# Scores of tiles 2 to 7 built on the bank's last tile from differences of key blocks, in a two-layer attention kernel on one core

## The chip, the cores and the metric

One core of a Trainium2 chip runs the whole program. The metric is the device time of one execution in microseconds; the median of the runs is given. The engines named here are TensorE (PE, with its weight loads as PEld), VectorE (DVE), ScalarE (ACT), GpSimd (POOL) and SyncE (SP), which issues most transfers. Each engine works through its own list of instructions in order; semaphores tie the lists together.

## The reference

Four images of 64 channels and 32 x 32 positions go through two layers. Each layer is a group norm, a single-head self-attention over the 1024 positions, and a residual:

```python
h = group_norm(x, norm_w, norm_b)             # 32 groups
q, k, v = h @ Wq + bq, h @ Wk + bk, h @ Wv + bv
scores = einsum('bnc,bmc->bnm', q, k) * C ** (-0.5)   # C = 64
attn = softmax(scores, axis=-1)
x = x + (einsum('bnm,bmc->bnc', attn, v) @ Wo + bo)
```

## The kernel before

A unit is one image in one layer: UNITS = 8, and LAST = 7. The 1024 positions are held as two halves of 512 (HALF), one half in partitions 0 to 63 and the other in 64 to 127, with the channels along the partitions. The scores of a unit are made transposed, 128 keys by 1024 queries at a time: TILES = 8 tiles, each filling two PSUM banks (left: queries of one half, right: of the other). JS = 4 blocks of 128 positions make a half.

The projection (`project`, L741) puts queries and keys of one half into each of two buffers: `front` holds queries of the first half in its upper 64 partitions and keys of it in its lower, `back` keys of the second half above and queries below. So that queries and keys stand in the same partitions, SP copies halves of them into `cross` (`swap_hi`, `swap_lo`). Products are made in a reduced float format; to keep the precision, each operand is split in a high part (written by ScalarE, L389 to L398) and a low part, the rest (VectorE, L557 and L564; for units 0 and 1 GpSimd, L307). A tile of scores (`scores_main`, L791) is three pairs of matmuls, high by high, high by low and low by high; a pair works on the upper and the lower 64 rows of the array, for the left and the right bank.

To each tile a fourth pair (`scores_row`, L821) adds the row of negated maxima, `q_row`, through a matrix of ones, so that the exponential on ScalarE (`exp`, L440) finds scores less the query's maximum. The maxima come one unit ahead: while unit w has its scores made, `next_max(w, m)` (L724) makes one plain high-by-high product for unit w+1, `part` (L571) on VectorE reduces it over keys, `join` (L595) takes the last step, `turn_max` (L783) transposes the result on TensorE, `stage_max` copies it, and SP puts it in `q_row` (`place_rows`, L240).

The order is written out by hand for each engine. One pass w over the steady loop:

- TensorE (L950): `next_max` and `scores` of tiles 0 to 7 in turn, the denominators of unit w-1 (L865), `values` (probabilities by values, L833) of tiles 0 to 4, a wait for `rden_done`, `turn_max(w+1)`, values 5 and 6, `project(w+2)`, `project_v(w+2)`, values 7. Two score buffers alternate, so tile t waits for exponential t-2. The last unit (L986) has three buffers and no maxima to make.
- VectorE (L687): the eight reductions `part`, with `first_add` (sum of probabilities of tiles 0 and 1) among them, `join`, statistics of unit w+2 (`own_stats`, `share_stats`, `join_stats`), the reciprocal of unit w-1's denominators, `affine`, `low_front` and `low_back` of unit w+2.
- ScalarE (L478): eight exponentials, the norm, `stage_max`, `bias_x`, `high_front`, `high_back`, `copy_v`, `copy_attn`.
- GpSimd (L344): the sums of probabilities of tiles 2 to 7 (`add`, L317), with `root` (L301, for the norm of unit w+2) after the third of them, and `finish(w-1)` before the last.
- SP (L274): spread of the reciprocal, `place_rows`, then the four `cross` transfers of unit w+2.

Of the kernel before, what the change touches and what calls it, by code (L numbers as in the profile page):

```python
# [11 lines left out]
P = 128  # L12
# [18 lines left out]
def attention_pair(nc, x, layer_params, consts, out):  # L31
# [14 lines left out]
    JS = HALF // P  # L46
    POOL_ADDS = TILES - 2
# [4 lines left out]
    with ExitStack() as ctx:  # L52
# [13 lines left out]
        back_w = [sb(f"back_w{n}", [P, P]) for n in range(LAYERS)]  # L66
        back_bias = [sb(f"back_bias{n}", [P, 1]) for n in range(LAYERS)]
# [17 lines left out]
        front = [sb(f"front{b}", [P, N], F32R) for b in range(RING)]  # L85
        back = [sb(f"back{b}", [P, N], F32R) for b in range(RING)]
        cross = [sb(f"cross{b}", [P, N], F32R) for b in range(RING)]
        full_front = sb("full_front", [P, HALF])
        full_back = sb("full_back", [P, HALF])
# [33 lines left out]
        back_set = sem("back_set")  # L123
# [10 lines left out]
        front_hi = sem("front_hi")  # L134
        back_hi = sem("back_hi")
        front_full = sem("front_full")
        back_full = sem("back_full")
        front_lo = sem("front_lo")
        back_lo = sem("back_lo")
        first_back_hi = sem("first_back_hi")  # L140
        head_front_lo = sem("head_front_lo")
        head_back_lo = sem("head_back_lo")
# [3 lines left out]
        hi_swapped = [sem(f"hi_swapped{b}") for b in range(RING)]  # L146
        lo_swapped = [sem(f"lo_swapped{b}") for b in range(RING)]
# [40 lines left out]
        def low_count(later, head, unit):  # L188
            return (head, unit + 1) if unit < HEAD else (later, unit + 1 - HEAD)
# [7 lines left out]
        HI, LO = slice(0, HALF), slice(HALF, N)  # L197

        def back_hi_of(unit):
            return (back_hi, unit) if unit else (first_back_hi, 1)  # L200
# [13 lines left out]
        def scores_buffer(unit, t):  # L214
            return ps_scores[t % 2] if unit < LAST else (ps_scores[0], ps_scores[1], ps_max)[t % 3]
# [4 lines left out]
        def _(sp):  # L220
# [4 lines left out]

            def swap_hi(u):
                t = cross[u % RING]
                sp.wait_ge(front_hi, u + 1)
                sp.dma_start(t[0:C, HI].bitcast(F32), front[u % RING][C:P, HI].bitcast(F32)).then_inc(hi_swapped[u % RING], 16)
                sp.wait_ge(*back_hi_of(u))  # L230
                sp.dma_start(t[C:P, HI].bitcast(F32), back[u % RING][0:C, HI].bitcast(F32)).then_inc(hi_swapped[u % RING], 16)

            def swap_lo(u):
                t = cross[u % RING]
                sp.wait_ge(*low_count(front_lo, head_front_lo, u))
                sp.dma_start(t[0:C, LO].bitcast(F32), front[u % RING][C:P, LO].bitcast(F32)).then_inc(lo_swapped[u % RING], 16)
                sp.wait_ge(*low_count(back_lo, head_back_lo, u))
                sp.dma_start(t[C:P, LO].bitcast(F32), back[u % RING][0:C, LO].bitcast(F32)).then_inc(lo_swapped[u % RING], 16)
# [32 lines left out]
            for u in range(2):  # L271
                swap_hi(u)
                swap_lo(u)
            for w in range(UNITS):  # L274
                if 0 < w < LAST:
                    spread_rden(w - 1)
                if w + 1 < UNITS:
                    place_rows(w + 1)
                if w == LAST:
                    spread_rden(w - 1)  # L280
                if w + 2 < UNITS:
                    swap_hi(w + 2)
                    swap_lo(w + 2)
                if w > B:
                    store(w - 1 - B)
# [4 lines left out]
        def _(pool):  # L290
# [16 lines left out]
            def low_parts(u):  # L307
                pool.wait_ge(front_hi, u + 1)
                pool.wait_ge(front_full, u + 1)
                pool.tensor_tensor(front[u][:, LO], full_front[:, :], front[u][:, HI].bitcast(F32),  # L310
                                   ALU.subtract).then_inc(head_front_lo, 1)
                pool.wait_ge(*back_hi_of(u))
                pool.wait_ge(back_full, u + 1)
                pool.tensor_tensor(back[u][:, LO], full_back[:, :], back[u][:, HI].bitcast(F32),
                                   ALU.subtract).then_inc(head_back_lo, 1)
# [26 lines left out]
            low_parts(0)  # L342
            low_parts(1)
# [9 lines left out]
        def _(act):  # L353
# [6 lines left out]
            def set_back(n):  # L360
                act.wait_ge(params_in[n], 16)
                low = slice(C, P)
                act.activation(back_w[n][low, 0:C], layer[n][low, WK:WK + C], ACT.Copy)
                act.activation(back_w[n][low, C:P], layer[n][low, WQ:WQ + C], ACT.Copy)
                act.activation(back_bias[n][0:C, :], layer[n][low, BIAS_QK:BIAS_QK + 1], ACT.Copy)
                act.activation(back_bias[n][low, :], layer[n][0:C, BIAS_QK:BIAS_QK + 1], ACT.Copy).then_inc(back_set, 1)
# [22 lines left out]
            def high_front(u):  # L389
                act.wait_ge(params_in[u // B], 16)  # L390
                act.wait_ge(proj_mm, u + 1)
                act.activation(front[u % RING][:, HI], projected(u)[:, HI], ACT.Identity,  # L392
                               bias=layer[u // B][:, BIAS_QK:BIAS_QK + 1]).then_inc(front_hi, 1)

            def high_back(u):
                act.wait_ge(back_set, u // B + 1)
                act.activation(back[u % RING][:, HI], projected(u)[:, LO], ACT.Identity,
                               bias=back_bias[u // B][:, :]).then_inc(back_hi, 1)  # L398

            def whole_front(u):  # L400
                if u:
                    act.wait_ge(head_front_lo, u)
                act.activation(full_front[:, :], ps_scores[0][:, HI], ACT.Identity,
                               bias=layer[u // B][:, BIAS_QK:BIAS_QK + 1]).then_inc(front_full, 1)

            def whole_back(u):
                if u:
                    act.wait_ge(head_back_lo, u)
                else:
                    act.wait_ge(first_back_hi, 1)  # L410
                act.wait_ge(back_set, u // B + 1)
                act.activation(full_back[:, :], ps_scores[0][:, LO], ACT.Identity,
                               bias=back_bias[u // B][:, :]).then_inc(back_full, 1)
# [47 lines left out]
            set_back(0)  # L461
            apply_norm_first()
            high_front(0)
            whole_front(0)
            whole_back(0)
            apply_norm(1)
            copy_v(0)
            set_back(1)
            high_front(1)
            high_back(1)  # L470
            whole_front(1)
            whole_back(1)
# [5 lines left out]
            for w in range(UNITS):  # L478
                prep = w + 2 < UNITS
                for t in range(TILES):  # L480
                    exp(w, t)
                if prep:
                    apply_norm(w + 2)
# [573 lines left out]
```

## Time and profile before

| | |
|---|---|
| median of 3 runs | 180.64 us (180.60 to 180.78) |
| the profiled execution | 180.29 us, of which the span is 178.5 |
| TensorE, VectorE, GpSimd, ScalarE busy | 96%, 78%, 67%, 57% of the span |
| a steady unit | 20.06 us |

The page gives each engine's busy time as a share of the span. A timeline lists instructions by start and duration in us, a run of like ones in one row ("x8" with the time from the first start to the last end); in square brackets stands how long the engine had been idle, and whose work ended that. Matmuls follow each other before the one in front has ended, so the spacing of their starts, not their duration, is what each costs. VectorE and ScalarE instructions overlap by about 0.1 us in the same way.

### The profile page before, as it was taken

To read this page: it belongs to the slowest core of one execution; us is meant where nothing else is said; L and a number is where in the kernel's file an instruction comes from. 1 tells how busy PE (TensorE), PEld (TensorE's weight loads), DVE (VectorE), ACT (ScalarE), POOL (GpSimd) and SP (SyncE) were. 2 spreads that over 40 slices of the span, in tenths; PEclk is the share of its full clock that TensorE was granted. 3 is DMA by queue.
4 is the path that set the end of the run, shared out by engine and by line. 5 is a ranking of instruction groups with operands and counts; after the bars stand their busy time and mean duration, and the time that the engine had idled before them with its cause. 6 is when DMAs were issued, how large, how long until landed. Compare 5 with 4: busy or idle time off the path is not lost.

```text
span 178.5 us, 3311 instructions
## 1 busy us (share of the span) xinstructions
PE 170.8 (96%) x1239; PEld 92.5 (52%) x1239; DVE 139.0 (78%) x201; ACT 102.6 (57%) x137; POOL 119.2 (67%) x78
## 2 busy tenths in 40 slices
PE   7868899999999999999999999999999999999992
PEld 3425575247632665247632665247632665358671
DVE  2799899539993899739992899739992899979943
ACT  3479388257923786167923786167923786039400
POOL 3265029893889879888889879888889879700000
PEclk9999999999999999999999999999999999999999
DMA  5544200004001500034001500034001510113011
GB/s 147 207 88 92 59 0 0 2 19 105 0 4 46 130 3 4 0 74 103 4 0 48 128 5 0 0 76 107 0 0 49 131 62 0 32 33 102 16 62 59
DMA packets 6656, 8.90 MB, mean 50 GB/s; under 512 B 1208, under 2 KB 3696, under 8 KB 6640
## 3 DMA queue, kind: packets, MB, share of 16 engines
q1 hardware_dynamic: 6208, 8.23, 18.7%
q10 hardware_dynamic: 432, 0.46, 0.8%
q8 instruction: 10, 0.16, 0.4%
q14 instruction: 6, 0.05, 0.1%
HBM read 1.58 MB, written 1.05 MB: 15 GB/s over the span
## 4 chain that ended last, share of the span: by engine, by line
PE 88%; DVE 7%; DMA 1%; issue 1%; POOL 0%; ACT 0%; DVEq 0%; POOLq 0%
PE ps_both L846 28%; PE ps_scores L814 9%; PE ps_scores L830 8%; PE ps_scores L816 8%; PE ps_scores L818 8%; PE ps_max L771 5%; DVE part_max L576 4%; PE ps_both L853 4%; PE ps_scores L750 4%; PE ps_both L758 3%; PE ps_both L771 3%; PE ps_both L871 2%; PE ps_scores L771 2%; DMA xs<-x_dram 1%; PE ps_both L785 1%
## 5 line engine op out<-in xcount | busy, mean ns | idle before, releaser
L324 POOL TENSOR_TENSOR prob_sum<-prob_sum,probs 128x1024 f32<-128x1024 f32 x40 | 95.1, 2378 | 20.8 <-DVE prob_sum L606 17.6
L450 ACT ACTIVATE probs<-ps_scores 128x1024 f32<-128x1024 f32 x62 | 63.3, 1027 | 12.9 <-PE ps_scores L831 6.5
L846 PE MATMUL ps_both<-probs,vals 128*64 128x512 f32 x224 | 52.2, 598 | 0.0
L576 DVE TENSOR_REDUCE part_max<-ps_max 128x2 f32<-128x1024 f32 x32 | 39.1, 1223 | 1.1 <-PE ps_max L772 0.4
L846 PEld LDWEIGHTS ps_both<-probs,vals 128*64 128x64 f32 x224 | 14.6, 136 | 24.1 <-issue 23.0
L576 DVE TENSOR_REDUCE part_max<-ps_both 128x2 f32<-128x1024 f32 x21 | 25.7, 1224 | 0.8 <-PE ps_both L772 0.7
L830 PE MATMUL ps_scores<-q_row,ones_r 64*128 64x512 f32 x62 | 24.4, 393 | 0.5 <-ACT q_row L432 0.5
L831 PE MATMUL ps_scores<-q_row,ones_r 64*128 64x512 f32 x62 | 24.4, 394 | 0.0
L559 DVE SCALAR_TENSOR_TENSOR front<-ps_scores,layer,front 128x512 fp32r<-128x512 f32 x6 | 4.5, 750 | 23.5 <-ACT front L392 23.5
L381 ACT ACTIVATE h<-xs,shift,gain 128x512 f32<-128x512 f32 x7 | 5.7, 811 | 26.8 <-DVE shift L543 26.8
L576 DVE TENSOR_REDUCE part_max<-ps_scores 128x2 f32<-128x1024 f32 x11 | 13.4, 1223 | 1.1 <-PE ps_scores L772 1.1
L830 PEld LDWEIGHTS ps_scores<-q_row,ones_r 64*128 64x128 f32 x62 | 11.4, 184 | 3.2 <-issue 0.7
L614 DVE RECIPROCAL quarter_rden<-ps_both 128x256 f32<-128x256 f32 x7 | 12.2, 1750 | 1.0 <-PE ps_both L871 1.0
L814 PE MATMUL ps_scores<-front,back 64*128 64x512 f32 x31 | 12.9, 415 | 0.0
L815 PE MATMUL ps_scores<-back,cross 64*128 64x512 f32 x31 | 12.8, 414 | 0.0
L815 PE MATMUL ps_scores<-back,front 64*128 64x512 f32 x31 | 12.3, 398 | 0.0
L814 PE MATMUL ps_scores<-front,cross 64*128 64x512 f32 x31 | 12.3, 398 | 0.0
L818 PE MATMUL ps_scores<-front,back 64*128 64x512 f32 x31 | 12.1, 391 | 0.0
L819 PE MATMUL ps_scores<-back,front 64*128 64x512 f32 x31 | 12.1, 391 | 0.0
L819 PE MATMUL ps_scores<-back,cross 64*128 64x512 f32 x31 | 12.1, 391 | 0.0
L818 PE MATMUL ps_scores<-front,cross 64*128 64x512 f32 x31 | 12.1, 391 | 0.0
L817 PE MATMUL ps_scores<-back,front 64*128 64x512 f32 x31 | 12.1, 390 | 0.0
(161 smaller groups left out, 393.8 us busy)
## 6 DMA issues: line engine op xcount, KB each, us to landing
cross<-front SPq DMA_DIRECT2D x16, 128.0 KB, 2.3
cross<-back SPq DMA_DIRECT2D x16, 128.0 KB, 2.3
rden<-quarter_rden SPq DMA_DIRECT2D x28, 64.0 KB, 2.1
xs<-x_dram SPq DMA_DIRECT2D x4, 256.0 KB, 4.7
out_dram<-xs SPq DMA_DIRECT2D x3, 256.0 KB, 3.2
q_row<-max_rows SPq DMA_DIRECT2D x14, 2.0 KB
layer<-layers_dram SPq DMA_DIRECT2D x1, 194.5 KB, 2.7
layer<-layers_dram ACTq DMA_DIRECT2D x1, 194.5 KB, 4.7
```

The costliest lines, as they stand in the source:

```text
L324: pool.tensor_tensor(total[:, :], total[:, :], probs[t][:, :], ALU.add).then_inc(added, 1)
L450: act.activation(probs[t][:, :], scores_buffer(u, t)[:, :], ACT.Exp, scale=SCALE).then_inc(exp_done, 1)
L576: dve.tensor_reduce(part_max[u % 2][:, at:at + 2 * JS + 1:2 * JS], ps[:, :].rearrange("p (g n) -> p g n", g=2), AX.X, ALU.max, negate=True ...
L771: pe.matmul(ps[:, HI], f[top, tile], (x if crossed else g)[top, HI], start=True, stop=True)
L814: pe.matmul(left, key_top[top, hi], front_u[top, HI], start=True, stop=False)
L815: pe.matmul(right, key_low[low, hi], back_u[low, HI], start=True, stop=False)
L816: pe.matmul(left, key_top[top, hi], front_u[top, LO], start=False, stop=False)
L818: pe.matmul(left, key_top[top, lo], front_u[top, HI], start=False, stop=False)
L819: pe.matmul(right, key_low[low, lo], back_u[low, HI], start=False, stop=False)
L830: pe.matmul(left, ones_r[top, :], row[top, :], start=False, stop=True)
L831: pe.matmul(right, ones_r[low, :], row[low, :], start=False, stop=True).then_inc(scores_mm, 1)
L846: mm = pe.matmul(ps_attn[half * C:(half + 1) * C, :], v, probs[t][:, cols], start=(t == 0), stop=(t == TILES - 1))
```

## The change

Softmax of a query does not change when a tile's scores are taken as the last tile's scores plus a product with the difference of two key blocks. From unit 1 on, tiles 0 and 1 are made as before (anew, with the row of maxima). Tiles 2 to 7 start from what the bank still holds, the tile two back, and add the product of the queries with the difference between their key block and that one: three pairs of matmuls with no start flag, and no fourth pair. Tiles now alternate between the two halves of the keys, from the last block down (`key_block`).

For this, keys and queries get buffers of their own: `q_hi`, `q_lo`, `k_hi` and `k_lo` hold both halves, queries or keys of the first half in one set of 64 partitions and of the second in the other; `x_hi` and `x_lo` hold the keys exchanged. `k_hi` and `x_hi` have 384 columns more (DIFF = HALF - P) for the differences. `project` makes four products of 64 rows by 64 columns in place of two of 64 by 128. ScalarE makes one more copy per unit, `whole_keys` (keys in full precision), and `high_differences` after the exponentials. VectorE makes `key_differences` (384 columns) in place of `low_back`, and, one pass later and just ahead of the reciprocal, `low_keys`. SP moves the exchange of the low parts to the next pass, ahead of the reciprocal's spread, and adds the exchange of the differences. The last unit has two score buffers in place of three, and its values are set between its scores. Unit 0 keeps its row of maxima in all tiles.

```diff
@@ SP
-            for u in range(2):
-                swap_hi(u)
-                swap_lo(u)
+            def swap_hi(u):
+                sp.wait_ge(*k_hi_of(u))
+                exchange(x_hi[u % RING], k_hi[u % RING], HI, hi_swapped[u % RING])
+            def swap_differences(u):
+                sp.wait_ge(d_hi_set, u)
+                exchange(x_hi[u % RING], k_hi[u % RING], DIFFS, d_swapped[u % RING])
+            def swap_lo(u):
+                sp.wait_ge(*k_lo_of(u))
+                exchange(x_lo[u % RING], k_lo[u % RING], HI, lo_swapped[u % RING])
...
+            swap_hi(0)
+            swap_lo(0)
+            swap_hi(1)
             for w in range(UNITS):
+                if w + 1 < UNITS:
+                    swap_differences(w + 1)
+                    swap_lo(w + 1)
                 if 0 < w < LAST:
                     spread_rden(w - 1)
...
                 if w + 2 < UNITS:
                     swap_hi(w + 2)
-                    swap_lo(w + 2)
@@ ACT
+            def whole_keys(u):
...
+                act.activation(k_full[u % 2][:, HI], projected(u)[:, LO], ACT.Identity,
+                               bias=bias_k[u // B][:, :]).then_inc(k_full_set, 1)
+            def high_differences(u):
+                act.wait_ge(*diff_of(u))
+                act.activation(k_hi[u % RING][:, DIFFS], k_full[u % 2][:, DIFFS], ACT.Copy).then_inc(d_hi_set, 1)
...
                 for t in range(TILES):
                     exp(w, t)
+                if w < LAST:
+                    high_differences(w + 1)
                 if prep:
                     apply_norm(w + 2)
...
-                    high_front(w + 2)
-                    high_back(w + 2)
+                    high_queries(w + 2)
+                    high_keys(w + 2)
+                    whole_keys(w + 2)
                     copy_v(w + 2)
@@ DVE
+            def key_differences(u):
+                full = k_full[u % 2]
+                dve.wait_ge(k_full_set, u + 1)
+                dve.scalar_tensor_tensor(out=full[:, DIFFS], in0=projected(u)[:, HALF:HALF + DIFF],
+                                         scalar=bias_k[u // B][:, :], in1=full[:, P:HALF],
+                                         op0=ALU.add, op1=ALU.subtract).then_inc(diff_set, 1)
+            def low_keys(u):
+                dve.wait_ge(k_hi_set, u)
+                dve.wait_ge(d_hi_set, u)
+                dve.tensor_tensor(k_lo[u % RING][:, :], k_full[u % 2][:, CHAIN], k_hi[u % RING][:, CHAIN].bitcast(F32),
+                                  ALU.subtract).then_inc(k_lo_set, 1)
...
                     join_stats(w + 2)
+                low_keys(w + 1)
                 if w:
                     reciprocal(w - 1)
                 if prep:
                     affine(w + 2)
-                    low_front(w + 2)
-                    low_back(w + 2)
+                    low_queries(w + 2)
+                    key_differences(w + 2)
@@ PE
-                pe.matmul(projected(u)[:, HI], p[first, 0:P], h[first, :], start=True, stop=True)
-                pe.wait_ge(back_set, u // B + 1)
-                pe.matmul(projected(u)[:, LO], back_w[u // B][second, :], h[second, :], start=True, stop=True).then_inc(proj_mm, 1)
+                pe.matmul(ps[TOP, HI], p[TOP, wq], h[TOP, :], start=True, stop=True)
+                pe.matmul(ps[LOW, HI], p[LOW, wq], h[LOW, :], start=True, stop=True)
+                pe.matmul(ps[LOW, LO], p[TOP, wk], h[TOP, :], start=True, stop=True)
+                pe.matmul(ps[TOP, LO], p[LOW, wk], h[LOW, :], start=True, stop=True).then_inc(proj_mm, 1)
...
             def scores(u, t):
                 scores_main(u, t)
-                scores_row(u, t)
+                if u == 0 or t < 2:
+                    scores_row(u, t)
...
+                product(left, top_hi[TOP, hi], q_hi[b][TOP, :], anew, False)
+                product(right, low_hi[LOW, hi], q_hi[b][LOW, :], anew, False)
+                product(left, top_hi[TOP, hi], q_lo[b][TOP, :], False, False)
+                product(right, low_hi[LOW, hi], q_lo[b][LOW, :], False, False)
+                product(left, top_lo[TOP, lo], q_hi[b][TOP, :], False, not anew)
+                mm = product(right, low_lo[LOW, lo], q_hi[b][LOW, :], False, not anew)
+                if not anew:
+                    mm.then_inc(scores_mm, 1)
...
-            for t in range(TILES):
+            for t in range(4):
                 scores(LAST, t)
             pe.wait_ge(rden_done, LAST)
             values(LAST, 0)
             values(LAST, 1)
+            scores(LAST, 4)
+            scores(LAST, 5)
             values(LAST, 2)
             values(LAST, 3)
-            denominators_last()
+            scores(LAST, 6)
+            scores(LAST, 7)
             values(LAST, 4)
             values(LAST, 5)
+            denominators_last()
             spread_last()
             values_last(0)
             values_last(1)
```

## Rows read from the trace of the kernel before

**Rows 1.** The page: busy time, share of the span, instructions of each engine.

```profile
PE 170.8 (96%) x1239; PEld 92.5 (52%) x1239; DVE 139.0 (78%) x201; ACT 102.6 (57%) x137; POOL 119.2 (67%) x78
```

**Rows 2.** Timeline, VectorE, one steady unit: start, duration, instruction, idle time before.

```profile
60.30 1.23 DVE L576 TENSOR_REDUCE part_max<-ps_max 128x2 f32<-128x1024 f32 x1
...
63.76 1.22 DVE L606 TENSOR_TENSOR prob_sum<-probs 128x1024 f32<-128x1024 f32 x1
64.89 1.22 DVE L576 TENSOR_REDUCE part_max<-ps_both 128x2 f32<-128x1024 f32 x1
...
69.80 1.23 DVE L576 TENSOR_REDUCE part_max<-ps_scores 128x2 f32<-128x1024 f32 x1 [0.16 <-PE ps_scores L772]
71.06 0.17 DVE L599 TENSOR_REDUCE neg_max<-part_max 128x8 f32<-128x16 f32 x1
...
73.00 1.75 DVE L614 RECIPROCAL quarter_rden<-ps_both 128x256 f32<-128x256 f32 x1
...
78.83 0.75 DVE L559 SCALAR_TENSOR_TENSOR front<-ps_scores,layer,front 128x512 fp32r<-128x512 f32 x1 [3.87 <-ACT front L392]
79.50 0.74 DVE L566 SCALAR_TENSOR_TENSOR back<-ps_scores,back_bias,back 128x512 fp32r<-128x512 f32 x1
80.36 1.23 DVE L576 TENSOR_REDUCE part_max<-ps_max 128x2 f32<-128x1024 f32 x1
```

**Rows 3.** Timeline, TensorE, the same unit.

```profile
60.80 0.39 PE L830 MATMUL ps_scores<-q_row,ones_r 64*128 64x512 f32 x1
...
61.03 0.39 PE L771 MATMUL ps_both<-back,front 64*128 64x512 f32 x1
...
70.26 4.51 PE L846 MATMUL ps_both<-probs,vals 128*64 128x512 f32 x20
74.80 0.27 PE L785 MATMUL ps_both<-const_sb,neg_max 128*8 128x128 f32 x1
...
76.87 0.69 PE L750 MATMUL ps_scores<-h,layer 64*128 64x512 f32 x1
...
77.93 1.09 PE L758 MATMUL ps_both<-wvo,h 128*64 128x128 f32 x16
```

**Rows 4.** Timeline, ScalarE, the same unit.

```profile
61.24 9.15 ACT L450 ACTIVATE probs<-ps_scores 128x1024 f32<-128x1024 f32 x8 [0.77 <-PE ps_scores L831]
...
78.11 0.69 ACT L392 ACTIVATE front<-ps_scores,layer 128x512 fp32r<-128x512 f32 x1 [1.49 <-PE ps_scores L752]
78.69 0.68 ACT L397 ACTIVATE back<-ps_scores,back_bias 128x512 fp32r<-128x512 f32 x1
```

**Rows 5.** Timeline, GpSimd and VectorE, unit 6.

```profile
145.40 9.92 POOL L324 TENSOR_TENSOR prob_sum<-prob_sum,probs 128x1024 f32<-128x1024 f32 x4 [1.28 <-DVE prob_sum L606]
...
153.11 3.29 DVE L630 TENSOR_TENSOR late_sum<-probs 128x1024 f32<-128x1024 f32 x1
```

**Rows 6.** Timeline, GpSimd, the steady unit.

```profile
65.11 7.44 POOL L324 TENSOR_TENSOR prob_sum<-prob_sum,probs 128x1024 f32<-128x1024 f32 x3 [1.24 <-DVE prob_sum L606]
73.04 0.55 POOL L305 TENSOR_TENSOR rstd<-var_eps,minus_half 128x1 f32<-128x1 f32 x1 [0.48 <-DVE var_eps L530]
```

**Rows 7.** Timeline, the last unit, all engines.

```profile
158.50 0.50 PE L814 MATMUL ps_scores<-front,cross 64*128 64x512 f32 x1
...
159.74 1.95 ACT L450 ACTIVATE probs<-ps_scores 128x1024 f32<-128x1024 f32 x2 [1.09 <-PE ps_scores L831]
...
166.07 3.67 PE L853 MATMUL ps_both<-probs,vals 128*64 128x256 f32 x32
...
169.51 0.69 DVE L652 TENSOR_TENSOR attn<-attn,rden 128x512 f32<-128x512 f32 x1
...
170.88 0.96 DVE L616 RECIPROCAL block_rden<-ps_max 128x128 f32<-128x128 f32 x1
...
172.53 1.04 PE L895 MATMUL ps_max<-block_rden,const_sb 128*64 128x128 f32 x16
```

## What the change is predicted to do, and why

> **What bounds the kernel now.** I read the page first, then the timelines of one steady unit (from 60 to 80 us), engine by engine, then the last two units. TensorE is 96% busy and VectorE 78% [rows 1], so the page alone says that TensorE matmuls taken away are time won. The unit says otherwise. Follow VectorE from the first reduction of one unit to the first of the next [rows 2, 3, 4]: reductions and the first add 60.30 to 71.06 (10.76 us), join and statistics to 73.00 (1.94), reciprocal until TensorE may turn the maxima at 74.80 (1.80), two value tiles until the projection at 76.87 (2.07), projection until ScalarE's first copy at 78.11 (1.24), copies and low parts until the next first reduction at 80.36 (2.25): 20.06 us, one closed loop. TensorE's own work is as long: its five value tiles end at 70.26 + 4.51 = 74.77, just when the turn (held by rden_done) is released [rows 3]. Whoever shortens one of the two only meets the other.
>
> **What TensorE gains.** A pair of row matmuls takes the slot from 60.80 to 61.03, 0.23 us [rows 3]. Six tiles lose it: 6 x 0.23 = 1.39 us per unit. Tiles 2 to 7 still wait for the exponential two tiles back, and the eight exponentials, 9.15 us now [rows 4], come somewhat faster. So TensorE reaches the turn about 1 us earlier, and is then held there by the reciprocal.
>
> **What VectorE's loop gains and loses, per unit.**
> - Reductions: now and then they wait for TensorE, 0.16 us in front of the last one [rows 2]; that is the least gain. The spacing of operations that wait for nothing is 1.13 us (63.76 to 64.89). Eight at that and 1.26 for the last (69.80 to 71.06) make 10.30: at most 0.46 gained. I take 0.35, since TensorE will be ahead nearly everywhere.
> - low_keys is new, between the statistics and the reciprocal, so in the loop. Two SBUF inputs of 512 columns: half of the 1.13 of the 1024-column add is 0.57, and the spacing of the present low part of 512 columns is 0.67 (78.83 to 79.50) [rows 2]. I take 0.60, with nobody in its way (below).
> - key_differences takes low_back's place, but waits for k_full, a third ScalarE copy. Copies follow at 0.58 (78.11, 78.69) [rows 4]: the third starts at 79.27, and with 0.68 ends at 79.95. A column costs about 1 ns (1.13 us for 1024), so 384 columns cost 0.13 less than 0.67, and reductions can start at 79.97 + 0.54 = 80.51 for 80.36: +0.15 (0 to +0.3).
> - The same copy pushes copy_v and copy_attn back, behind which next_max 1 and the first exponential stand: copy_attn ends at 78.11 + 4 x 0.58 + 0.60 = 81.03, and next_max 1 comes some 1.2 us after the first reduction's matmuls, at about 81.1. Nothing, with little to spare.
> - high_differences runs on ScalarE after the last exponential (61.24 + 9.15 = 70.39), when it idles; d_hi is there before VectorE asks at 73.0. Nothing.
> - SP: the exchanges of differences and low keys now stand ahead of the reciprocal's spread and of the q_row transfers. low_keys ends 1.75 us before the reciprocal does, time for two issues, and some 6 us remain until scores read what they bring. Nothing.
> - Projection: four 64x64 matmuls for two 64x128. The present two, on different rows, run together: 76.87 to 77.93, 1.06 us for both in two passes. Value matmuls, on different columns, run together too: 20 in 4.51, 0.23 each, where one projection pass takes 0.53 [rows 3]. No row shows rows and columns both split. Bounds: 0 (four at once) and +1.06 (two pairs in turn). I take 0, since each of the four has its own quarter of the array.
>
> By the Trainium skill ("TensorEngine Tiling (Array Packing)", Tiling Modes) 64x64 gives four independent tiles, but its Gotcha 1 (PSUM Pressure) says that different row tiles cannot access one PSUM bank at once, and the two query products do write one bank. No row here has that pattern; by that rule the projection would take at least a turn more, as in rival 3.
>
> Sum: -0.35 + 0.60 + 0.15 + 0 = +0.40 us per unit.
>
> **The port between VectorE and GpSimd.** The one present operation of VectorE with two SBUF inputs that meets a GpSimd add in full is the tail's pair sum: 3.29 us from 153.11 to 156.40, while four GpSimd adds run from 145.40 to 155.32 [rows 5]; the same shape takes 1.22 elsewhere [rows 2]. 155.32 + 1.08 = 156.40: it was not slowed down, it waited for the add to end. low_keys is such an operation. In a steady unit GpSimd's third add ends at 72.55 and its root starts at 73.04 [rows 6]; low_keys would start where the reciprocal does now, at 73.00 [rows 2]. With the reductions 0.35 shorter it comes 9.24 - 0.35 = 8.9 us after first_add's start, the third add ends 8.8 us after it, and root, set off by the same statistics, still follows some 0.04 behind low_keys. It slips in and root waits for it, which costs nothing: root has time till the reciprocal is over. So 0.60 stands, but by a hair.
>
> The Trainium skill ("SBUF — State Buffer", SBUF: two separate sides) calls this an exclusive lock, held by whichever of a two-input VectorE operation and a GpSimd operation starts first. The tail row agrees (a wait of 2.2 us); by that rule, too, low_keys is first by 0.04 us.
>
> **The ends.** Head and unit 0: VectorE's reductions follow each other there as before, low_keys runs ahead of a norm that is not last, and only the +0.15 stays. Units 1 to 5: 5 x 0.40 = 2.0. Unit 6 has no statistics, so low_keys falls into the third of its four adds (2.48 each) [rows 5] and waits for its end at 152.84 + 0.15; it then holds the fourth up by 0.6, to 156.1. The pair sum (1.08) and the tail add (1.22) follow, so denominators and scores come about 0.6 late, 0.15 of it counted: +0.45. Last unit [rows 7]: six row pairs gone, -1.39; two buffers for three, so tile 2 waits for exponential 0 (159.74 + 1.03 + 0.07 = 160.84, +0.38) and tile 3 for exponential 1 (161.69, +0.22). Value tiles 4 and 5 now stand ahead of the denominators, and nothing covers the reciprocal. From the first score: tiles 0 to 3 end at 3.95, value tiles 0 and 1 (3.67 for four) at 5.8, scores 4 and 5 at 7.2, value tiles 2 and 3 at 9.0; exponential 6 starts 0.9 later and ends at 10.9. The last late add ends at 12.15, finish_tail takes 1.37 (169.51 to 170.88), the reciprocal 0.96: the spread starts at 14.5, for 172.53 - 158.50 = 14.03 now: +0.5 net.
>
> Total: 0.15 + 2.0 + 0.45 + 0.5 = +3.1 us. The sum is made on the profiled execution, 180.29 us with a span of 178.5; the median of the runs is 180.64, 0.35 more, and a difference carries over: 180.64 + 3.1 = 183.7. With the bounds but port and projection: +0.11 to +0.8 per unit and 0.2 to 1.3 at the ends, so 181.5 to 185.9.
>
> **Rivals.**
> 1. GpSimd first at the port. For it: 0.04 us decides. If root (0.55 [rows 6]) gets in, low_keys waits for it: +0.55 in five units, 2.75, 186.5 us. If the add behind root gets in too, 0.55 + 2.48 per unit: 5 x 3.0 and about 4 in units 0 and 6, some 203 us. Against the second: VectorE is already waiting when the port falls free.
> 2. Faster: the reductions follow TensorE, so their stretch shrinks by the full 1.39. Then -1.39 + 0.60 + 0.15 = -0.64 per unit, -3.2, with +1.1 at the ends 178.5 us. It decides once the stretch loses over 0.75 us, that is when eight spacings fall to 1.09 us. For it: the spacings look like TensorE's tile, five pairs of 0.23. Against it: the add at 63.76 to 64.89 waits for no maxima, and takes 1.13 as well.
> 3. The projection in two turns: +1.06 in six units, 6.4, so 190.1 us. For it: no row shows the pattern. Against it: column and row splits each run side by side.
> 4. That the change does not do what it says can only mean that tiles 2 to 7 get no shorter, because the wait for the exponential holds them. TensorE has slack at the turn, so the time is the forecast's.
>
> **How the numbers follow.** Forecast 50% (183.7, from 181.5 to 185.9); rival 1 short 17%, long 5%; rival 3 14%; rival 2 9%; gains and losses cancel, 5%. A measurement of this kernel tells about 0.2%, 0.36 us, from no change. Faster 9%, same 5%, slower 86%. The forecast, short rival 1 and rival 3 hold 81%: 181.5 to 190.2.
>
> **What the profile will show.** TensorE idle about 1 us ahead of the turn, released by the reciprocal; low_keys at 0.6 us between mean_gain and reciprocal (near 1.2: root was first; over 3: an add was); the projection's slot at 1.06 or at 2.1; a period near 20.5 us; reductions 1.13 apart without waits; TensorE idle ahead of the last spread. A period under 20.06 us, or a turn that the reciprocal doesn't release, would make the prediction wrong.

## The result and the profile after

The changed kernel takes 185.05 us (median of 4 runs, 184.82 to 185.17) where the kernel before, run beside it, takes 180.71 (180.60 to 180.88): a ratio of 1.0242, with a 95% interval of 1.0222 to 1.0263. It is slower by 4.3 us, and the forecast was +3.1 (183.7, range 181.5 to 190.2). The profiled execution took 184.93 us with a span of 183.1, 4.6 more than the span of before.

The page of the changed kernel, busy time by engine and the shares of the chain that ended last. TensorE was 96% busy [rows 1] and is 91%, and VectorE now carries half of the chain, where TensorE carried 88% of it:

```profile
PE 166.4 (91%) x1187; PEld 84.9 (46%) x1187; DVE 141.8 (77%) x208; ACT 106.8 (58%) x150; POOL 121.5 (66%) x78
...
DVE 50%; PE 29%; issue 8%; ACT 6%; DMA 2%; SPq 2%; POOL 0%; DVEq 0%; ACTq 0%; POOLq 0%
```

The chain of the kernel before, for comparison:

```profile
PE 88%; DVE 7%; DMA 1%; issue 1%; POOL 0%; ACT 0%; DVEq 0%; POOLq 0%
```

Timeline, VectorE, the same steady unit as [rows 2]:

```profile
61.04 1.22 DVE L623 TENSOR_REDUCE part_max<-ps_max 128x2 f32<-128x1024 f32 x1
...
71.46 0.17 DVE L646 TENSOR_REDUCE neg_max<-part_max 128x8 f32<-128x16 f32 x1
...
73.40 0.81 DVE L615 TENSOR_TENSOR k_lo<-k_full,k_hi 128x512 fp32r<-128x512 f32 x1
74.13 1.75 DVE L661 RECIPROCAL quarter_rden<-ps_both 128x256 f32<-128x256 f32 x1
...
81.10 0.62 DVE L608 SCALAR_TENSOR_TENSOR k_full<-ps_scores,bias_k,k_full 128x384 f32<-128x384 f32 x1 [0.40 <-ACT k_full L447]
81.63 1.21 DVE L623 TENSOR_REDUCE part_max<-ps_max 128x2 f32<-128x1024 f32 x1
```

Timeline, TensorE, the same unit, to be read against [rows 3]:

```profile
70.35 4.51 PE L910 MATMUL ps_both<-probs,vals 128*64 128x512 f32 x20
75.93 0.27 PE L834 MATMUL ps_both<-const_sb,neg_max 128*8 128x128 f32 x1 [1.07 <-DVE quarter_rden L661]
76.14 1.94 PE L910 MATMUL ps_both<-probs,vals 128*64 128x512 f32 x8
78.00 0.64 PE L798 MATMUL ps_scores<-h,layer 64*64 64x512 f32 x1
78.01 0.64 PE L799 MATMUL ps_scores<-h,layer 64*64 64x512 f32 x1
78.02 0.64 PE L800 MATMUL ps_scores<-h,layer 64*64 64x512 f32 x1
78.03 0.64 PE L801 MATMUL ps_scores<-h,layer 64*64 64x512 f32 x1
...
79.02 1.09 PE L807 MATMUL ps_both<-wvo,h 128*64 128x128 f32 x16
```

The value tiles end at 74.86, and then TensorE stands idle for 1.07 us until the reciprocal lets it turn the maxima: most of the time of the six row pairs lies here (the second run below puts it back). VectorE's loop reads, against before: first reduction to join 10.42 us for 10.76 (-0.34), join to reciprocal 2.67 for 1.94 (+0.73; +0.60 a unit later, where low_keys takes 0.60), reciprocal to projection 3.87 for 3.87, projection to first reduction 3.63 for 3.49 (+0.14). In the unit shown low_keys takes 0.81 because GpSimd's third add still runs until 73.65. Over the four steady units from 61.04 to the first reduction of unit 6 at 143.01 the period is 20.49, for 20.07 before.

The port between VectorE and GpSimd, one unit later: low_keys and the root of the next norm (for [rows 6]). low_keys starts 0.04 us ahead; the root, 0.55 before, takes 1.05:

```profile
93.97 0.68 DVE L615 TENSOR_TENSOR k_lo<-k_full,k_hi 128x512 fp32r<-128x512 f32 x1
94.57 1.75 DVE L661 RECIPROCAL quarter_rden<-ps_both 128x256 f32<-128x256 f32 x1
```

```profile
94.01 1.05 POOL L335 TENSOR_TENSOR rstd<-var_eps,minus_half 128x1 f32<-128x1 f32 x1
```

In unit 0 the root is first, by 0.15 us, and neither of the two takes longer (GpSimd, then VectorE):

```profile
33.91 0.55 POOL L335 TENSOR_TENSOR rstd<-var_eps,minus_half 128x1 f32<-128x1 f32 x1 [0.53 <-DVE var_eps L572]
```

```profile
34.06 0.68 DVE L615 TENSOR_TENSOR k_lo<-k_full,k_hi 128x512 fp32r<-128x512 f32 x1
```

GpSimd's last add of a unit and VectorE's first_add of the next: the add ends at 85.06, and first_add starts at 85.13.

```profile
82.66 2.40 POOL L360 TENSOR_TENSOR prob_sum<-prob_sum,probs 128x1024 f32<-128x1024 f32 x1
```

```profile
85.13 1.22 DVE L653 TENSOR_TENSOR prob_sum<-probs 128x1024 f32<-128x1024 f32 x1
```

The ends (for [rows 5] and [rows 7]). VectorE in unit 6, where low_keys and the pair sum wait for adds of a run of four on GpSimd (148.07 to 158.25):

```profile
153.71 2.34 DVE L615 TENSOR_TENSOR k_lo<-k_full,k_hi 128x512 fp32r<-128x512 f32 x1
155.97 1.75 DVE L661 RECIPROCAL quarter_rden<-ps_both 128x256 f32<-128x256 f32 x1
157.63 1.70 DVE L677 TENSOR_TENSOR late_sum<-probs 128x1024 f32<-128x1024 f32 x1
```

SP issues the last unit's row of maxima behind the four spreads:

```profile
160.30 1.31 SPq L274 DMA_DIRECT2D q_row<-max_rows  x2
```

TensorE in the last unit: first score, first row of maxima, tile 2, the first value run, the first scores behind it, the spread:

```profile
161.27 0.49 PE L875 MATMUL ps_scores<-q_hi,x_hi 64*128 64x512 f32 x1
...
162.69 0.49 PE L893 MATMUL ps_scores<-q_row,ones_r 64*128 64x512 f32 x1 [0.46 <-DMA q_row<-max_rows]
...
164.40 0.47 PE L875 MATMUL ps_scores<-q_hi,x_hi 64*128 64x512 f32 x1 [0.28 <-ACT probs L489]
...
166.13 1.95 PE L917 MATMUL ps_both<-probs,vals 128*64 128x256 f32 x16
168.01 0.50 PE L875 MATMUL ps_scores<-q_hi,x_hi 64*128 64x512 f32 x1
...
177.10 1.09 PE L959 MATMUL ps_max<-block_rden,const_sb 128*64 128x128 f32 x16 [1.08 <-DVE block_rden L663]
```

So the 4.6 us of span lie at four landmarks: the first reduction of unit 1 comes 0.48 later (40.70 for 40.22), units 1 to 5 add 1.95 (the first reduction of unit 6 is at 143.01 for 140.58, +2.43 in all), unit 6 adds 0.34 (first score of the last unit 161.27 for 158.50, +2.77 in all), and the last unit takes 15.83 us from first score to spread where it took 14.03: +1.80.

### The profile page after: what moved, and what is told of

The parts are those of the page before. It is cut to its first block, busy times and chain, and to the rows that moved or that the text cites. A ratio compares the mean times of both kernels' runs of the same rounds, so it can differ in the third digit from the quotient of the medians.

```text
span 183.1 us, 3264 instructions
## 1 busy us (share of the span) xinstructions
PE 166.4 (91%) x1187; PEld 84.9 (46%) x1187; DVE 141.8 (77%) x208; ACT 106.8 (58%) x150; POOL 121.5 (66%) x78
## 3 DMA queue, kind: packets, MB, share of 16 engines
HBM read 1.58 MB, written 1.05 MB: 14 GB/s over the span
## 4 chain that ended last, share of the span: by engine, by line
DVE 50%; PE 29%; issue 8%; ACT 6%; DMA 2%; SPq 2%; POOL 0%; DVEq 0%; ACTq 0%; POOLq 0%
DVE part_max L623 28%; PE ps_both L910 9%; PE ps_scores L875 6%; DVE quarter_rden L661 6%; DVE prob_sum L653 4%; PE ps_scores L798 4%; PE ps_both L917 4%; DVE stats L551 2%; ACT q_hi L429 2%; ACT k_full L447 2%; DVE k_full L608 2%; DVE k_lo L615 2%; DMA xs<-x_dram 2%; SPq L284 1%; PE ps_max L820 1%
## 5 line engine op out<-in xcount | busy, mean ns | idle before, releaser
L875 PE MATMUL ps_scores<-q_hi,k_hi 64*128 64x512 f32 x64 | 27.6, 431 | 1.1 <-ACT probs L489 1.1
L875 PE MATMUL ps_scores<-q_hi,x_hi 64*128 64x512 f32 x64 | 27.5, 430 | 0.3 <-ACT probs L489 0.3
L875 PE MATMUL ps_scores<-q_hi,x_lo 64*128 64x512 f32 x64 | 25.0, 391 | 0.0
L875 PE MATMUL ps_scores<-q_hi,k_lo 64*128 64x512 f32 x64 | 25.0, 391 | 0.0
L875 PE MATMUL ps_scores<-q_lo,k_hi 64*128 64x512 f32 x64 | 25.0, 390 | 0.0
L875 PE MATMUL ps_scores<-q_lo,x_hi 64*128 64x512 f32 x64 | 24.9, 390 | 0.0
L875 PEld LDWEIGHTS ps_scores<-q_hi,k_hi 64*128 64x128 f32 x64 | 11.7, 183 | 8.1 <-ACT probs L489 7.4
L875 PEld LDWEIGHTS ps_scores<-q_hi,x_lo 64*128 64x128 f32 x64 | 11.8, 184 | 1.2
L875 PEld LDWEIGHTS ps_scores<-q_hi,k_lo 64*128 64x128 f32 x64 | 11.8, 184 | 1.1
L875 PEld LDWEIGHTS ps_scores<-q_lo,x_hi 64*128 64x128 f32 x64 | 11.9, 185 | 0.4
```

Source lines behind the costliest of these rows:

```text
L875: return pe.matmul(out, keys, queries, start=start, stop=stop, skip_group_check=True)
```

## The experiments

In each run the kernel before ran beside it, at 180.5 to 180.9 us in the median. A period below is the mean of the four units between the first reductions of units 2 and 6. The edits are shown in part, with the lines that matter.

### 1 and 2: lengthen VectorE's loop, give TensorE its work back

```diff
@@ low_keys(u), first run: one reduction of 512 columns ahead of it
+                dve.tensor_reduce(spare[:, :], k_full[u % 2][:, HI], AX.X, ALU.max)
```

> The changed kernel with one more VectorE operation ahead of low_keys: a maximum over 512 columns of k_full (one SBUF input, result unused), some 0.6 us. Theory: the VectorE loop (reductions, statistics, low_keys, reciprocal, turn, projection, copies, back to the reductions) sets the period, so units 1 to 5 get 0.6 us longer each and unit 6 up to 0.6: 185.05 + 3.0 to 3.6 = 188.1 to 188.7 us, period 21.05. Rival, that TensorE or ScalarE sets the period and low_keys lies in a gap: 185.0 to 185.5.

Measured: 189.41 us (1.0487, 1.0456 to 1.0518). The period is 21.05, +0.56 for an operation of 0.60, as expected. The rest, some 1.5 us, came in unit 0: there low_keys, 0.6 later than in the changed kernel, found GpSimd's next add running and waited for it.

The first run, VectorE, then GpSimd, unit 0:

```profile
34.73 2.68 DVE L618 TENSOR_TENSOR k_lo<-k_full,k_hi 128x512 fp32r<-128x512 f32 x1
```

```profile
34.50 7.63 POOL L361 TENSOR_TENSOR prob_sum<-prob_sum,probs 128x1024 f32<-128x1024 f32 x3
```

What is put into VectorE's loop is paid nearly in full (0.56 of 0.60), and rival 1's long price (0.60 becomes 2.68) is real once low_keys comes 0.2 us after the start of an add.

```diff
@@ scores(u, t), second run: the fourth pair is back, with zeros for ones in tiles 2 to 7
-                if u == 0 or t < 2:
-                    scores_row(u, t)
+                scores_row(u, t, ones_r if u == 0 or t < 2 else zero_r)
```

> The changed kernel with the fourth pair of matmuls put back in tiles 2 to 7 of units 1 to 7, with zeros in place of the ones, so that it adds nothing: TensorE's saving is undone, all else stays. Theory: TensorE idles 1.1 us ahead of each turn, so 1.39 us more fill that gap; 0.3 us of it shows, and the reductions get back up to 0.35 us of waiting: +0.3 to +0.65 in units 1 to 6 and +1.39 in the last, 188.2 to 190.4 us. Rival, that TensorE's time counts in full: +1.39 in seven units, 194.8 us.

Measured: 188.59 us (1.0446, 1.0409 to 1.0484); period 20.87, +0.38 for 1.39 us of TensorE work a unit. So of the time that the change takes from TensorE, 1.0 us a unit is worth nothing where it lies; the reductions (10.82 us in place of 10.42) take all that does count.

### 3 and 8: the reciprocal ahead of the statistics

```diff
@@ DVE, both runs (SP: the spread ahead of the low keys' exchange)
                 join(w + 1, neg_max[:, :])
+                if w:
+                    reciprocal(w - 1)
                 if prep:
                     own_stats(w + 2)
...
                 low_keys(w + 1)
-                if w:
-                    reciprocal(w - 1)
@@ POOL, run 8 alone: the last add ahead of finishing unit w-1
-                    if t == 6 and 0 < w < LAST - 1:
+                    if t == 7 and 0 < w < LAST - 1:
                         finish(w - 1)
```

> The changed kernel with VectorE's reciprocal straight after the join, ahead of the statistics and low_keys, and SP's spread of it ahead of the exchange of the low keys. Theory: the turn is then free when TensorE comes, some 1.1 us sooner; the norm, which now waits for the reciprocal's 1.75 and for low_keys, becomes what the projection waits for, some 0.45 us sooner than now: -2.2 in five units, and the last unit's row of maxima comes in time (-0.6): 182.2 to 182.9 us. If the projection followed the turn alone: 185.05 - 5 x 1.0 = 180 us. Rival, that the turn's wait hides behind something else: 185 us.

Measured: 188.48 us (1.0434, 1.0398 to 1.0471), slower by 3.4 than the changed kernel: the gain that was expected did not come. The turn was free when TensorE came, but the statistics, and behind them the root and GpSimd's adds, came later by the reciprocal's length, and first_add met GpSimd's last add. VectorE, two units of the third run, then GpSimd:

```profile
64.41 2.41 DVE L653 TENSOR_TENSOR prob_sum<-probs 128x1024 f32<-128x1024 f32 x1
...
85.63 2.44 DVE L653 TENSOR_TENSOR prob_sum<-probs 128x1024 f32<-128x1024 f32 x1
```

```profile
76.12 1.05 POOL L335 TENSOR_TENSOR rstd<-var_eps,minus_half 128x1 f32<-128x1 f32 x1 [1.42 <-DVE var_eps L572]
...
84.60 2.40 POOL L360 TENSOR_TENSOR prob_sum<-prob_sum,probs 128x1024 f32<-128x1024 f32 x1
```

first_add takes 2.44 in place of 1.22: it starts at 85.63, waits until the add of 84.60 is over at 87.00, and ends 1.07 later. The eighth run keeps the order and moves that add.

> Reciprocal ahead of the statistics as in the third run (188.48 us), and GpSimd's last add of a unit ahead of the two operations that finish the unit before. New theory of that run's loss: later statistics made the root and GpSimd's chain late, so that first_add stood 1.2 us before the port until the last add ended. With the add ahead of the wait for the spread reciprocal, the add ends about 3 us sooner, and first_add meets at most one of the short ones: first_add at 1.2 to 1.5 instead of 2.44 us, period 20.2 to 20.4, 183.3 to 184.6. Rival (the order on VectorE itself costs it, the port nothing): period 21.2, 188.5.

Measured: 182.74 us (1.0118, 1.0087 to 1.0149), 5.7 below the third run with one line of GpSimd's list moved; first_add is back at 1.21 to 1.27, the period 20.06, a little better than expected. That period is the one of the kernel before, and what holds it is the norm: VectorE waits 0.44 us for the root in each unit, since low_keys got in ahead of it (GpSimd, then VectorE):

```profile
74.57 1.05 POOL L335 TENSOR_TENSOR rstd<-var_eps,minus_half 128x1 f32<-128x1 f32 x1 [0.45 <-DVE var_eps L572]
```

```profile
75.65 0.21 DVE L583 TENSOR_SCALAR gain<-rstd,layer 128x1 f32<-128x1 f32 x1 [0.44 <-POOL rstd L335]
```

### 5: low_keys taken away

```diff
@@ low_keys(u)
-                dve.tensor_tensor(k_lo[u % RING][:, :], k_full[u % 2][:, CHAIN], k_hi[u % RING][:, CHAIN].bitcast(F32),
-                                  ALU.subtract).then_inc(k_lo_set, 1)
+                dve.memset(k_lo[u % RING][:, 0:1].bitcast(F32), 0.0).then_inc(k_lo_set, 1)
```

> The changed kernel with low_keys taken away: the low parts of keys and differences are zero in units 1 to 7 (cleared once at the start), and VectorE only sets one column to zero in its place, so nothing of it needs the port. Theory (low_keys' 0.60 us stands in VectorE's loop, and in unit 6 it waits at the port and makes the row of maxima late): period 20.45 - 0.6 = 19.85 us, the same 0.6 in unit 0, the root back at 0.55; unit 6's reciprocal of unit 5 starts about 2.3 us sooner after join, the row is there when the last unit's first tile wants it, -0.6. Together about -4.5: 180.2 to 181.2. Rival (GpSimd's chain of adds or TensorE is the real bound, and low_keys stands in a gap that something else keeps open): period above 20.2 us and 183 us or more.

Measured: 181.27 us (1.0042, 1.0018 to 1.0067). The period is 19.93, so low_keys costs 0.56 a unit; the last unit takes 15.10, with the row there in time. Without low_keys the steady unit is a little shorter than before's 20.07. In unit 0, where 0.6 was expected, low_keys costs nothing: from the join of the maxima to the first reduction of unit 1 it takes 8.77 us with it and without it. That reduction came at 41.00 for 40.70 because the join itself came 0.30 later (32.23 for 31.93); whether the added clearing at the start did that is not shown.

### 6: the third copy

```diff
@@ ACT
-                    high_keys(w + 2)
                     whole_keys(w + 2)
+                    high_of_whole(w + 2)     # rounds k_full in SBUF
```

> The changed kernel with ScalarE's second and third copies exchanged: the keys in full precision come first, the high part is rounded from them in SBUF. Theory (key_differences waits 0.40 us for the third copy, and that is the +0.15 of each unit): it starts right behind the low queries, some 0.5 us sooner, and the first reduction is then held only by TensorE's first maxima product; -0.15 to -0.2 us per unit, period 20.25 to 20.30, six units: 184.0 to 184.3. Rival (the first reduction follows TensorE anyway): 185.05, period 20.45.

Measured: 186.61 us (1.0329, 1.0297 to 1.0361); period 20.74, worse by 0.25. key_differences did start behind the low queries, but the first maxima product needs the high part of the keys, which now comes last:

```profile
81.44 0.61 DVE L612 SCALAR_TENSOR_TENSOR k_full<-ps_scores,bias_k,k_full 128x384 f32<-128x384 f32 x1
82.66 1.23 DVE L627 TENSOR_REDUCE part_max<-ps_max 128x2 f32<-128x1024 f32 x1 [0.61 <-PE ps_max L825]
```

Both readings of the +0.14 were too simple: two chains meet at the first reduction, and the order of the copies only chooses which is late.

### 4 and 7: the last unit

```diff
@@ run 4: all tiles of the last unit anew, with the row and three buffers, values behind all scores
-                anew = u == 0 or t < 2
+                anew = u in (0, LAST) or t < 2
@@ run 7: SP, unit 6
-                if 0 < w < LAST:
+                if 0 < w < LAST - 1:
                     spread_rden(w - 1)
                 if w + 1 < UNITS:
                     place_rows(w + 1)
+                if w == LAST - 1:
+                    spread_rden(w - 1)
```

> The changed kernel with the last unit undone: all its tiles made anew with the row of maxima, three score buffers and the old order of scores, values and denominators. Theory: the last unit took 15.83 us from first score to spread in place of 14.03, 0.6 of it by the late row of maxima, which stays: 15.83 becomes 14.65, -1.2, 183.9 us. Rival, that the lost time there comes from late transfers alone: 185.0 us.

Measured: 184.50 us (1.0217, 1.0174 to 1.0260), and the last unit takes 14.75 (162.02 to 176.77), 1.08 less: as expected in the unit. The total shows half of it: in the profiled execution the first reduction of unit 1 came at 41.47 (40.70 in the changed kernel), though the run changes nothing in the head.

> The changed kernel with one exchange in SP's list, in unit 6 alone: the row of maxima of the last unit goes out ahead of the spread of unit 5's reciprocal. Theory (the row, behind four spreads, holds the last unit's first tile by 0.6 us): TensorE's idle time ahead of the first row product goes to 0, last unit from first score to spread 15.83 - 0.6 = 15.2 us, 184.4 to 184.6. Unit 5's output and the reciprocal of unit 6 come about 1.9 us later, with room. Rival (two buffers and the exponentials hold the last unit, and the late row only fills a wait that is there anyway): 185.0, last unit 15.8.

Measured: 185.12 us (1.0266, 1.0208 to 1.0323): no gain. The row came in time and tile 2 started at 163.69 for 164.40, but the spread of unit 5's reciprocal, now last, held the reciprocal of unit 6 until 164.00 (161.88 before the move), and VectorE's late adds became the bound:

```profile
164.00 1.76 DVE L663 RECIPROCAL quarter_rden<-ps_both 128x256 f32<-128x256 f32 x1 [3.40 <-DMA rden<-quarter_rden]
...
168.27 6.54 DVE L695 TENSOR_TENSOR prob_sum<-prob_sum,probs 128x1024 f32<-128x1024 f32 x5
```

The expectation had said "with room". In the fifth and the eighth run, where row and reciprocal both come early, the last unit takes 15.10 and 15.13: the late row is worth 0.7 of its 1.80, and the fourth run puts the other 1.1 on two buffers, the interleaved order and anew against chained tiles together, without telling them apart.

### 9 to 12: use TensorE's idle time

```diff
@@ PE, runs 9 to 12 (run 12: in the kernel before); the POOL line of run 8 in 9, 11 and 12
+                values(w, 5)
+                values(w, 6)
                 if w:
                     pe.wait_ge(rden_done, w)
                 turn_max(w + 1)
-                values(w, 5)
-                values(w, 6)
@@ run 11 alone: the fourth run's last unit, and in unit 6 the reciprocal and its spread
@@ ahead of low_keys and their exchange
```

> The changed kernel with two moves in hand-written order: TensorE does value tiles 5 and 6 ahead of the turn of the maxima (they fill the 1.07 us in which it waited for the reciprocal), and GpSimd adds its last tile ahead of finishing the unit before. Theory (TensorE's gain lies idle ahead of the turn, and the reciprocal holds the projection only through the order turn, value tiles, projection): turn at about 76.7 on the scale of the unit at 61.04, projection right behind, 1.0 us sooner; period 19.4 to 19.8 us, 5 units, 181.0 to 182.0. Rival (GpSimd's chain of six adds, root and two finishing operations takes the bound over, its loop is 19.8 to 20.4): 182.5 to 184.5.

Measured: 181.24 us (1.0020, 1.0002 to 1.0037), 3.8 below the changed kernel; period 19.83, just above what was expected. TensorE, the ninth run: no wait at the turn, and the projection now waits for the norm, 0.28 us here and about 0.15 in the units behind.

```profile
69.32 6.23 PE L910 MATMUL ps_both<-probs,vals 128*64 128x512 f32 x28
75.48 0.27 PE L834 MATMUL ps_both<-const_sb,neg_max 128*8 128x128 f32 x1
76.03 0.64 PE L798 MATMUL ps_scores<-h,layer 64*64 64x512 f32 x1 [0.28 <-ACT h L418]
```

From join to projection it takes 5.53 us in place of 6.54; 0.36 of that goes back at the port, where first_add takes 1.58 behind GpSimd's finishing operation, which runs from 62.43 to 63.72:

```profile
63.22 1.58 DVE L653 TENSOR_TENSOR prob_sum<-probs 128x1024 f32<-128x1024 f32 x1
```

GpSimd's move alone was not run; first_add waits for nothing in the steady units of the changed kernel (1.21), so these rows show nothing there for it to win.

> The same with TensorE's move alone, GpSimd's order left as in the changed kernel. Theory (first_add then comes 1 us sooner, while the last add, held behind the wait for the spread reciprocal, still runs): first_add waits at the port for 0.9 to 1.2 us in each unit, as in the third run, period 20.2 to 20.5, 184.0 to 185.2: the gain of the move is given back. Rival (first_add gets the port at no cost): as in the run before, 181 to 182.

Measured: 184.37 us (1.0196, 1.0158 to 1.0234), period 20.29. Without GpSimd's move most of the gain is given back at the port, as expected: first_add takes 2.04. VectorE, then GpSimd:

```profile
63.93 2.04 DVE L653 TENSOR_TENSOR prob_sum<-probs 128x1024 f32<-128x1024 f32 x1
```

```profile
62.49 2.39 POOL L360 TENSOR_TENSOR prob_sum<-prob_sum,probs 128x1024 f32<-128x1024 f32 x1
...
66.11 4.92 POOL L360 TENSOR_TENSOR prob_sum<-prob_sum,probs 128x1024 f32<-128x1024 f32 x2 [1.23 <-DVE prob_sum L653]
```

> Both moves, the last unit made anew with its row of maxima and three buffers as in the fourth run, and in unit 6 the reciprocal of unit 5 ahead of low_keys. Theory: the gains add, since each was measured at another place: units as in the ninth run, last unit 15.83 - 1.08 - 0.70 = 14.05 us, so 1.8 below the ninth run: 179.0 to 180.3, a little under the kernel before (180.6). Rival (unit 6 is held by GpSimd's adds and the tail, and takes up what the last unit gains): 180.5 to 181.5.

Measured: 179.69 us (0.9942, 0.9919 to 0.9964), 0.6% below the kernel before. The period is 19.83 again, and the last unit 14.06 from first score to spread:

```profile
157.84 0.50 PE L886 MATMUL ps_scores<-q_hi,x_hi 64*128 64x512 f32 x1
...
171.90 1.04 PE L970 MATMUL ps_max<-block_rden,const_sb 128*64 128x128 f32 x16
```

> The kernel before with the same two moves as the ninth run (value tiles 5 and 6 ahead of the turn, last add ahead of the finish). Theory (there TensorE has no idle time ahead of the turn, its own work is as long as the loop): no gain, period 20.0 to 20.1, 180.4 to 181.0; the move only pays with the TensorE time that the change sets free. Rival (the move pays by itself): 178 or less.

Measured: 180.25 us (0.9964, 0.9938 to 0.9990): a small gain where none was expected, period 19.82. From the start of the value tiles to the projection TensorE needs 6.36 us (70.61 to 76.97) for 6.61 before (70.26 to 76.87): the turn between value tiles costs it 0.25 more than the turn behind them, and how much of that was a wait for the reciprocal is not resolved. So the moves have a part that does not need the change. Set against the ninth run, this is also a fair measure of the change itself, since both have the same two moves: the periods are 19.83 with the change and 19.82 without it, and the times 181.24 and 180.25. With these moves the change gains nothing in the steady unit, though TensorE's idle time is used, and the last unit (15.88 for 14.13) makes it the slower of the two. The intervals of the last two runs overlap: whether the changed kernel, with all moves, beats the kernel before with two of them is open.

## Why the prediction was right, and where it was off

**What bounds, and where TensorE's gain goes: right.** Two loops of equal length were read from [rows 2] and [rows 3]; shortening TensorE's alone left it 0.81 to 1.07 us idle ahead of the turn (predicted about 1), released by the reciprocal in all six turns that wait for it. The second run shows it from the other side, and the ninth, with GpSimd's move, takes the idle time and wins 3.8 us with it.

**The terms of the steady unit: right.** Reductions -0.34 (-0.35), low_keys +0.56 by the run without it (+0.60), the wait for the third copy +0.14 (+0.15), projection 0 (0). Units 1 to 5 came to +1.95 (+2.0). Of the third copy the prediction saw one chain; the sixth run shows a second one, through the high keys: made to come 0.71 us later there, they lengthen the period by 0.25, so an estimate from these two is that this chain ends some 0.45 us earlier in the changed kernel.

**The projection.** The four products start within 0.03 us of each other, and the slot from the first to project_v is 1.02 us, for 1.06 before: rival 3 is out. By the Trainium skill ("TensorEngine Tiling (Array Packing)", Gotcha 1: PSUM Pressure) different row tiles cannot access one PSUM bank at once; here two of them write the same bank on different partitions side by side, and the trace decides.

**The port: right by the 0.04 us that the prediction named**, in units 1 to 5. low_keys was first, the root waited (1.05 for 0.55), and this cost nothing there; in unit 2 low_keys itself waited for the end of the third add (0.81 for 0.68). The forecast hung on the 0.04 us less than the prediction says: rival 1's short price, 0.55 when the root is first, did not appear in unit 0, where the root started 0.15 us ahead and low_keys still took 0.68. In unit 6 low_keys waited 1.7 us for an add, as worked out. The third, eighth and tenth runs show that the port decides more than the prediction gave it: the same first_add costs 1.22, 2.04 or 2.44 us according to when it meets GpSimd's last add. In the changed kernel it starts 0.07 us behind the end of that add, so GpSimd's list is a third bound close behind the two loops, as the tenth run shows; the prediction did not name it.

**The ends: the last unit is the term that was mis-sized**, +1.80 for +0.5. The step that failed is the one on SP, "some 6 us remain until scores read what they bring. Nothing". It was worked out in a steady unit and carried to unit 6, where low_keys' wait at the port makes the reciprocal, the turn and the four spreads late, and the row of maxima stands behind them: SP issued it at 160.30, and it held the first tile, which cost the unit 0.7 us. The other 0.6 builds up along the working from the first score. In the eighth run, where the row is in time, tiles 0 to 3 end at 4.15 us (predicted 3.95), the first value run at 6.03 (5.8), scores 4 and 5 at 7.63 (7.2), the second run at 9.51 (9.0), and the spread starts at 15.13 (14.5): value runs take 1.88 for 1.83, and the first pair of scores behind a run 0.34 for 0.23 (168.01 to 168.35 in the changed kernel). The prediction's two-buffer waits were right in kind (tile 2 waits for exponential 0).

**The head**, +0.48 for +0.15: 0.33 of it lies ahead of the join of the head's maxima (31.93 for 31.60) and can't be judged, since the same head gave 31.93 and 32.69 in the seventh and fourth runs. From there to the first reduction of unit 1 it takes 8.77 us for 8.62, the +0.15 of the prediction. Unit 6 gave +0.34 for +0.45.

**Rival 2 (faster)** needed reductions that follow TensorE. They ran at 1.13 us nearly without waits (10.42 us for the 10.30 of the working), as the add in [rows 2] had said.

## What to carry to other kernels

Where two engines have loops of equal length, taking work from one gives idle time at the point where they meet; find that wait, and look whether work that stands behind it can be moved ahead of it. Then try the same move without the change: here it brought the kernel before to the same period. A term worked out in a steady unit has to be worked out again in the units that lack one of its parts. Before an operation with two SBUF inputs is moved on VectorE, write down what GpSimd does at its new time, and which of GpSimd's operations can be moved out of its way.

## What the runs showed of the hardware

- Four fp32 matmuls of 64 rows by 64 columns, in the four quarters of the array, run together in the time of two of 64 by 128 (1.02 and 1.06 us in two passes), with two row tiles writing one bank, on different partitions.
- When VectorE waits for the port behind a run of GpSimd adds, it gets in between two queued adds: low_keys in unit 6 ended at 156.05, inside a run of four that lasted until 158.25 (in the first run, unit 0, at 37.41, inside a run of three until 42.13). The Trainium skill ("SBUF — State Buffer", SBUF: two separate sides) tells of an exclusive lock that goes to whoever starts first; these two rows agree, and add that the waiting engine is next.
- An operation on one column takes part in it, though the rows show it from one side only: the root went from 0.55 to 1.05 us when low_keys started 0.04 us ahead, while in unit 0 low_keys started 0.15 us behind the root, inside its 0.55, and still took 0.68. So the root did not hold the port to its end.
